# Gated cross-attention and mixture-of-experts layer, one core: where in the odd units GpSimd subtracts the row maxima of the first edge tile

## The reference, cut to what matters

```python
scores0 = jnp.einsum('bhqd,bhkd->bhqk', qh, kh)
bias = jnp.einsum('bhqd,dr->bhqr', qh, p_params)
d = jnp.clip(jnp.arange(Ql)[:, None] - jnp.arange(Kl)[None, :], -MAX_DIST, MAX_DIST) + MAX_DIST
rel = bias[:, :, jnp.arange(Ql)[:, None], d]
scores = scores0 + rel
causal = jnp.arange(Ql)[:, None] >= jnp.arange(Kl)[None, :]
scores = jnp.where(causal[None, None], scores, NEG_INF)
attn = jax.nn.softmax(scores, axis=-1)
```

## Time and profile before

| what | value |
|---|---|
| median of 3 runs | 698.43 us |
| the 3 runs | 698.43, 696.84, 702.94 us |
| the profiled execution's own time | 694.83 us |
| its span | 693.0 us |
| mean granted clock of PE in it | 0.941 of full speed |

### The profile page before, as it was taken

The page is one execution under the profiler, slowest core; times in us unless marked ns, Lnnn a source line. Parts: engine busy times, 40 slices in busy tenths (PEclk is TensorE's granted clock), DMA queues, the critical chain, the costliest instruction groups (busy, mean ns, idle before and its releaser), DMA issues.

```text
span 693.0 us, 10435 instructions
## 1 busy us (share of the span) xinstructions
PE 592.2 (85%) x3256; PEld 460.8 (66%) x3256; DVE 427.2 (62%) x868; ACT 268.8 (39%) x497; POOL 193.5 (28%) x186
## 2 busy tenths in 40 slices
PE   3446968888989797977579999999999999999996
PEld 3434635465656564642458888888888888888886
DVE  5187728765686749731674765738566575756553
ACT  3413546343824364635332424234232422434221
POOL 3162006400370035200203232322323232232222
PEclk9777989899989999999778999999999999999999
DMA  5944425325352615362212031220212122031220
GB/s 166 231 91 134 92 54 134 82 75 108 76 134 50 135 36 136 85 227 53 50 61 61 1 94 60 78 76 11 96 45 92 61 66 87 0 106 47 88 66 30
DMA packets 43600, 58.52 MB, mean 84 GB/s; under 512 B 8400, under 2 KB 25680, under 8 KB 43536
## 3 DMA queue, kind: packets, MB, share of 16 engines
q1 hardware_dynamic: 42608, 56.55, 30.3%
q10 hardware_dynamic: 960, 1.57, 1.1%
HBM read 33.13 MB, written 6.11 MB: 57 GB/s over the span
## 4 chain that ended last, share of the span: by engine, by line
PE 46%; issue 22%; DVE 13%; POOL 8%; DMA 6%; SPq 2%; ACT 2%; DVEq 0%; POOLq 0%; ACTq 0%
PE py L1542 8%; PE pg L1527 7%; PE pu L1527 7%; POOL hl L1234 4%; PE oT L993 4%; PE smax L930 4%; DMA qs<-mt 3%; PE oT L997 3%; PE sT L973 3%; DVE mx L662 2%; PE work L1008 2%; PE sT L972 2%; POOL d L456 2%; DVE mx L690 1%; DVE x L1421 1%
## 5 line engine op out<-in xcount | busy, mean ns | idle before, releaser
L1234 POOL TENSOR_TENSOR hl<-sg,hh 128x512 fp32r<-128x512 f32 x72 | 92.8, 1290 | 244.6 <-ACT hh L1277 229.1
L570 ACT ACTIVATE ex<-sT 128x512 f32<-128x512 f32 (+1 forms) x160 | 91.8, 593 | 136.6 <-PE sT L973 112.0
L1271 ACT ACTIVATE sg<-pg 128x512 f32<-128x512 f32 x72 | 43.1, 599 | 195.8 <-PE pu L1527 195.8
L662 DVE TENSOR_REDUCE mx<-smax 128x2 f32<-128x308 f32 x186 | 81.2, 474 | 30.3 <-PE smax L930 29.3
L1542 PE MATMUL py<-wxl,hh 128*128 128x256 f32 x288 | 81.4, 283 | 3.9 <-DVE x L1421 2.8
L1542 PE MATMUL py<-wxh,hl 128*128 128x256 f32 x288 | 80.5, 280 | 0.0
L1542 PE MATMUL py<-wxh,hh 128*128 128x256 f32 x288 | 80.3, 279 | 0.0
L1409 DVE TENSOR_TENSOR sg<-cwb,sg 128x512 f32<-128x512 f32 x64 | 60.3, 942 | 11.5 <-DMA cwb<-cwt_d 8.6
L1527 PE MATMUL pg<-x2l,wxh 128*128 128x512 f32 x144 | 60.8, 422 | 4.1 <-issue 4.1
L1542 PEld LDWEIGHTS py<-wxl,hh 128*128 128x128 f32 x288 | 54.2, 188 | 10.1 <-DVE x L1421 5.1
L930 PE MATMUL smax<-km,qs 96*128 96x316 f32 (+1 forms) x116 | 43.0, 398 | 20.7 <-DMA qs<-ql 9.1
(11 more groups left out here) (162 smaller groups left out, 1128.8 us busy)
## 6 DMA issues: line engine op xcount, KB each, us to landing
cwb<-cwt_d SPq DMA_DIRECT2D x64, 256.0 KB, 3.4
qs<-qh SPq DMA_DIRECT2D x56, 128.0 KB, 2.9
at<-rden_d SPq DMA_DIRECT2D x64, 64.0 KB, 2.3
out<-x SPq DMA_DIRECT2D x8, 512.0 KB, 4.4
ks<-km SPq DMA_DIRECT2D x16, 231.0 KB, 3.4
qs<-ql SPq DMA_DIRECT2D x28, 128.0 KB, 2.9
wx<-in_wx SPq DMA_DIRECT2D x9, 384.0 KB, 7.2
x<-in_x SPq DMA_DIRECT2D x3, 1024.0 KB, 8.6
```

The lines of the kernel that those rows point to most:

```text
L570: nc.scalar.activation(ex[:, g % 2, i % 5, q0:HALF], ST[i % 2][:, q0:HALF], ACT.Exp).then_inc(exp_s, 1)
L662: nc.vector.reduce_max(mx[:, p // NG if start else m_tile(h, p), stk::NSTK], banks[q % len(banks)][:, 0:PAIR].rearrange("p (j k) -> p j k" ...
L1234: nc.gpsimd.tensor_tensor(hl[:, i % R, :], sg[:, i % R, :], hh[:, i % R, :], ALU.subtract).then_inc(hl_done, 1)
L1271: nc.scalar.activation(sg[:, i % R, :], PG[i % RG][:], ACT.Silu).then_inc(sg_s, 1)
```

## The change: what it does

In `near`, the call of `subtract0` that stood behind the table of tile 0 is taken out, and the call at the end, which only `start` had, is now made always. In the odd units 1, 3 and 5 POOL therefore does: table of tile 0, wait for all copies of tile 1 (`sx_s`), table of tile 1 with its mask, and then `subtract0`. No instruction is added or taken away. The start of the kernel is the same as before.

```diff
                     ALU.mult).then_inc(d_s, 1)
-                if i == 0 and not start:
-                    subtract0()
-
             pool.wait_ge(d_s, 3 * b + 2)
             nc.gpsimd.tensor_tensor(d1[:], d1[:], con("causal1").unsqueeze(1).broadcast_to([P, H, 32]),
                                     ALU.add).then_inc(d_s, 1)
-            if start:
-                subtract0()
+            subtract0()
```

## The result

The changed kernel takes 701.75 us (median of 20 runs) against 698.2 us for the kernel before (20 runs). The ratio is 1.0054, with a 95% interval of 1.0028 to 1.0079: it is slower by 0.5%, or 3.8 us (2.0 to 5.5). One execution of the kernel before took 1965.14 us, in a slow state of the chip, and is left out of this ratio. The profiled execution took 701.71 us. The forecast was 699.6 us, within a range of 695.0 to 704.0, and a loss of 2.0 us. The loss is real, of the forecast's sign, and about twice its size.

A forecast was written before the change was run, and what follows sets the result against it. It took DVE to be held at the ends of units 1, 3 and 5 until POOL's edge work ended. Hold 1.85 plus clock 0.2, rounded to 2.0 us, on 697.6 gave 699.6 us, range 695.0 to 704.0.

The forecast's parts named there:

- DVE and POOL take turns, whole instructions at a time: Ends of units 1, 3 and 5: DVE's L703 is held until POOL's L434 ends; hold with small loss, chance 0.62.
- The timing inside unit 1: Unit 1's end: L434 runs from 120.09 to 123.73 us, so L703 ends at 123.77 instead of 123.17.
- The sum of the hold, 1.85 us: Ends of units 1, 3 and 5: L703 held behind L434 costs 0.60 + 0.58 + 0.67 = 1.85 us.
- PE's clock, "I take 0.2": Projection in units 1 and 5: longer PE gap could lower the clock, 1.2 us if in both; 0.2 taken.
- a sign of being wrong by the clock: Last copy of tile 1 to next L972, 13.7 us before: growth over 1.5 us would be the clock.
- The gain rival: Ends of units 1, 3 and 5: L434 doesn't hold L703, L705, L686; 6.3 us faster, 0.9%, chance 0.1.
- point of decision: L434 over about a microsecond later than 120.09, or DVE that much earlier, so L703, L705, L686 all precede it.
- The clock rival: PE at half speed through the projection and into the next unit's first items: 7.0 us slower, 1.0%, chance 0.08.
- The no-change rival: Unit ends: POOL's work has the same sum, DVE always waits for its last piece; -0.15 us, chance 0.2.

## Why the prediction was right, and where it was off

- **DVE and POOL take turns, whole instructions at a time.** Right, and shown: L703 took 3.0 us in all three units and ended 0.04 us behind L434. It shrank with half an L434, went with L434's place or absence, and the next instruction was held by a further one.
- **The timing inside unit 1.** L434 was to start 5.07 us behind the last copy of tile 1, which is 4.88 behind relc; it started 4.76 behind it (122.90 - 118.14). The first division was to take about 0.8 us; it took 0.78. L703 was to reach DVE's head 0.57 us behind L434's start; it was 0.65.
- **The sum of the hold, 1.85 us.** The edge stretches gave 1.89 in the first pair of profiles, but that they agree to 0.04 is luck. With PE kept busy the hold by itself is 1.42 to 1.58 us, 0.3 to 0.4 less than forecast (in unit 1 L703 ended 0.47 us later and not 0.60), and the rest was the clock.
- **PE's clock, "I take 0.2".** This term was mis-sized. The reason named with it was right: with the longer gap ahead of L942 the projection had the lower clock in all three units, and with the gap filled in none. It cost 0.47 us in the first pair of profiles, because L694 was nearly as late. In unit 1 it cost 1.2 us more in two of three profiles, and there the time from the last copy of tile 1 to the next unit grew by more than the 1.5 us that the prediction had named as a sign of being wrong by the clock.
- **What wasn't in the sum.** The forecast took it that a shift at a unit's end goes through to the end of the kernel one to one. It doesn't. The passage to the experts became 2.6 us longer in every profile that enters it as the changed kernel does, and 0.8 us of foreign delay did the same to the kernel before. The edge stretches' 1.9 and 2.6 make 4.5 us, inside the 2.0 to 5.5 measured; with the 1.2 us of unit 1 it would be 5.7 in some executions. That the forecast came within a factor of two is owed to the hold, which it had right, and not to this larger half of the loss, which it didn't have. Since the kernel before happens to stand just ahead of a step, a like change in another kernel could cost its hold alone.
- **The gain rival** (three times 2.1 us) priced the right quantity: without L434 the edge stretches are shorter by 2.3 us each. It had the wrong condition, since L434 was in the way. Its point of decision, L434 starting behind L686, is the kernel that beats both.
- **The clock rival** had the wrong place: not in the next unit's first items (the mean clock is 1.00 in the first 20 us of the passage in both kernels), but from 20 to 25 us on.
- **The no-change rival** was near for the local work: POOL's last piece ends 0.47 us later than it did, counted from relc, and not 0.07 sooner.

## What to carry to other kernels

When DVE and POOL share a resource, the place for a long POOL instruction is beside DVE instructions that aren't held (here the reductions and those that read PSUM), and not in front of a short one on the path; look for a short instruction whose recorded time is long and ends with the other engine's. A wait that keeps the long one back can be the better edit than an order that starts it sooner. And where PE runs with gaps, measure a change of a few microseconds by its own stretch as well as by the total, since the clock can add to it or swallow it somewhere else.

## What had not been expected of the hardware

- POOL is held as well. The forecast had counted on this in just these two places, from one held L451; here the sizes are seen: L454 takes 0.62 us beside a division instead of 0.30, and L462 1.43 instead of 1.09.
- A delay of 0.8 us lengthened a passage of 88 us by 2.7 to 2.9 us, and in a kernel with the long passage 2.5 us of matmuls moved the ratio from 1.0054 to 1.0059, which the intervals can't tell apart. In the longer passage PE was busy longer, at a granted clock of 0.83 instead of 0.88, and no other engine was.
- The chain of waits has no word for the hold. In the kernel before it shows as "issue", and in the changed one as time of the held instruction itself, `DVE nm L699`.
